# The second gathered quad of each pair waits for later products instead of the sum that frees its slot

## The chip, the core and the metric

The kernel runs on one core of one Trainium2 chip. The metric is the device time of one execution in microseconds (us), the median over several executions. TensorE (PE) multiplies matrices, VectorE (DVE) and ScalarE (ACT) work elementwise, GpSimd (POOL) here mostly issues gathers, SyncE (SP) issues the other DMAs.

## The reference, cut to what matters

A graph of 3125 nodes with 128 features and 50,000 edges goes through five gated steps and a normalisation, then through three edge layers and a second normalisation. The change lies in the edge layers, of which each does this:

```python
parts = [x[src], x[dst]]
if edge_attr is not None:
    parts.append(edge_attr)
e = relu(concatenate(parts, axis=-1) @ We + be)
agg = segment_sum(e * norm[:, None], dst, num_segments=3125)
x_new = relu(concatenate([x, agg], axis=-1) @ Wn + bn)
```

`edge_attr` is absent in the first edge layer and is the previous layer's `e` in the second and third. The last layer's `e` isn't needed by anybody.

## The kernel before

The products with the nodes' features are made once a layer (`p` for the source side, with the bias, `q` for the target side), so that an edge needs one row of `p`, one row of `q` and, from the second layer on, its own `e` times a 128x128 matrix. `edge_pass` then walks over the edges. An edge tile holds 128 edges, a quad is four tiles, and a pass has 115 quads, each in a slot of its own, numbered in order of time. Two kinds of quads alternate:

- 43 **sorted** quads: their rows of `p` come out of SBUF by a one-hot matmul (L1592).
- 72 **rest** quads, number `b` = 0 to 71: their rows of `p` are gathered from DRAM by GpSimd, four indirect DMAs a quad, one a tile, into one of `ROW_SLOTS` = 4 buffers `rows`, number `b % 4` (L1512).

The order of slots is sorted, rest, rest, over and over (36 triples), with one more sorted quad after every fifth triple, seven in all. So the rest quads come in pairs: an even `b`, called the first of a pair here, and an odd one, the second, in the next slot.

For the quad in slot `q`, TensorE does `products(q)`: the one-hot matmuls with `q_parts` (L1599), for a sorted quad the one with `p_sb` (L1592), and in the second and third pass the matmul with `before` (L1603). Its last matmul raises `spread`. For a rest quad VectorE adds the gathered rows (`add`, L1737; it waits for `spread` and for the gather's landing), ScalarE applies the relu (L1677). Two slots later TensorE does `turn_and_sum(q)`: in the first two passes it turns `e` for storing (L1614), and always it multiplies `e` by the weighted one-hot matrix (L1623); the last matmul raises `summed`. VectorE takes the sums into `agg_t` in `gather_up` (L1744). The order on TensorE is written out by hand:

```python
products(q, values)
if q >= LAG:
    turn_and_sum(q - LAG)
```

with `LAG` = 2. `summed` is therefore the last reader of a `rows` buffer, and GpSimd waits for it before it gathers the quad `b` into the buffer of `b - 4`. The first four quads of a pass wait for less. Each engine's instructions are executed in order; GpSimd's four gathers of a quad follow the wait without another. SyncE loads `before`, stores `after` and loads the rows for the sorted quads meanwhile.

Of the kernel before, what the change touches and what calls it, by code (L numbers as in the profile page):

```python
# [1370 lines left out]
def edge_pass(nc, tag, nth, Wc, psum, keep, t, is_first, p_dram, e_before, e_after, over_before,  # L1371
# [4 lines left out]
    with ExitStack() as ctx:  # L1376
# [3 lines left out]
        def sem(name):  # L1380
            return ctx.enter_context(nc.semaphore(name + tag))
# [3 lines left out]
        ROWS, BEFORE, AFTER, LOADED, PAIRS, OWN = ROW_SLOTS, 3, 3, 2, 2, 2  # L1385
# [29 lines left out]
        spread = sem("spread")  # L1415
# [45 lines left out]
        def slot_of(b):  # L1461

            return rest_slots[b]

        def lists(i, first, engine):

            end = 4 * QUAD if i < TRIPLES else 2 * QUAD
            _, values = nc.values_load_multi_w_load_instructions(
                keep["list_i"][0:1, i, first:end], engines=(engine,), min_val=0, max_val=WINDOWS - 1,
                skip_runtime_bounds_check_because="a window's number is a count of at most all the windows but one")  # L1470
            return values

        def overflow(engine):

            return nc.values_load(keep["over_i"][0:1, 0:1], engines=(engine,), min_val=0,
                                  max_val=ALL_TILES - SORT_TILES)
# [15 lines left out]
        @block.gpsimd  # L1492
        def _(pool):
            def further_rows():
                with pool.Fori(0, overflow(mybir.EngineType.Pool)) as i:
                    pool.wait_ge(over_hots_on, i * 4 + 4)
                    pool.sem_inc(over_gathering, 1)
                    nc.gpsimd.indirect_dma_start(
                        out=over_row, out_offset=None, in_=p_dram,
                        in_offset=bass.IndirectOffsetOnAxis(ap=over_src[:].bitcast(U32), axis=0),  # L1500
                    ).then_inc(over_row_in, 16)

            for b in range(REST_QUADS):
                if b == 1:
                    further_rows()
                if b >= ROWS:
                    pool.wait_ge(summed, slot_of(b - ROWS) + 1)
                elif b >= 2:
                    pool.wait_ge(spread, slot_of(b - 2))
                for m in range(QUAD):  # L1510
                    s = b * QUAD + m
                    nc.gpsimd.indirect_dma_start(  # L1512
                        out=rows[:, b % ROWS, m * D:(m + 1) * D], out_offset=None, in_=p_dram,
                        in_offset=bass.IndirectOffsetOnAxis(ap=t["src_i"][:, s:s + 1].bitcast(U32), axis=0),
                    ).then_inc(rows_in[b % ROWS], 16)
# [313 lines left out]
```

## Time and profile before

| what | us |
|---|---|
| median of 3 executions | 2675.99 |
| fastest and slowest of them | 2674.0 and 2693.58 |
| the profiled execution's own time | 2685.29 |
| span of its profile, first to last instruction | 2683.2 |

The profile comes from one execution, 9.3 us above the median. Its span begins with the tables, the adjacency and the gated steps, which the change doesn't touch. The three edge passes lie at about 962 to 1488, 1519 to 2066 and 2098 to 2640 us. In a timeline an instruction has its start, its duration, and in brackets the idle time of its engine just before it and what ended that. "remote" there is a semaphore whose raiser the profile doesn't name, "issue" is a time in which the engine waited for nothing that the profile shows. The end of a matmul is modelled.

### The profile page before, as it was taken

The numbers are of one execution on the slowest core, as the hardware profiler recorded it, in microseconds if no ns is written. First come the engines' busy times: TensorE is split into PE (matmuls) and PEld (weight loads), VectorE is DVE, ScalarE is ACT, GpSimd is POOL, SyncE is SP. The second block draws the span as 40 slices with busy tenths as digits, with TensorE's granted clock in tenths as the row PEclk, the third lists the DMA queues.
The fourth block names the chain that finished last, engine by engine and source line by source line (L and its number), as shares of the span: only waits on it lengthen the run. The fifth ranks groups of instructions, "written<-read, shape, count | busy, mean of one in ns | idle before, by whom it ended". The sixth has DMA issues, their size and how long they took to land. (4 is left out here: it accounts for less than half of the span.)

```text
span 2683.2 us, 48362 instructions
## 1 busy us (share of the span) xinstructions
PE 2142.4 (80%) x14264; PEld 1585.6 (59%) x14264; DVE 1447.8 (54%) x4661; ACT 653.0 (24%) x1271; POOL 1001.1 (37%) x1015
## 2 busy tenths in 40 slices
PE   7666679999999657777777678888888677888885
PEld 4222234444444347666666578787877577777774
DVE  6988832332332446656666455555555455555555
ACT  0246731221221122222222322222222211111111
POOL 0765400000000035555555245454553454555550
PEclk8777789999999768878888899999999888889887
DMA  2123550000000343333333255555553333433431
GB/s 81 25 57 83 95 47 1 0 0 0 0 0 0 120 127 107 116 102 114 105 112 108 83 164 160 154 164 165 162 162 117 103 101 97 112 105 106 112 106 38
DMA packets 193650, 242.15 MB, mean 90 GB/s; under 512 B 56276, under 2 KB 120047, under 8 KB 192799
## 3 DMA queue, kind: packets, MB, share of 16 engines
q1 hardware_dynamic: 161023, 172.73, 22.3%
q0 software_dynamic: 31840, 57.21, 9.1%
q10 hardware_dynamic: 576, 9.44, 0.9%
q8 instruction: 128, 2.10, 0.3%
q14 instruction: 83, 0.68, 0.1%
HBM read 149.75 MB, written 69.88 MB: 82 GB/s over the span
## 5 line engine op out<-in xcount | busy, mean ns | idle before, releaser
L1512 POOL DMA_INDIRECT rows<-p_dram,src_i x864 | 824.7, 954 | 751.9 <-PE psum L1623 441.8
L1744 DVE TENSOR_TENSOR agg_t<-psum,agg_t 128x128 f32 x1380 | 394.1, 286 | 466.6 <-remote 263.6
L1603 PE MATMUL psum<-w_c,before 128*128 128x128 f32 x1840 | 440.8, 321 | 24.2 <-issue 23.8
L1592 PE MATMUL psum<-p_sb,pair_src 128*128 x1032 | 257.7, 330 | 151.3 <-issue 85.6
L1677 ACT ACTIVATE rows<-rows 128x512 f32<-128x512 f32 x216 | 136.1, 630 | 901.1 <-DVE rows L1737 608.3
L893 PE MATMUL psum<-adj,parts 128*128 (+2 forms) x1750 | 339.7, 351 | 5.8 <-ACT agg L972 4.4
L1603 PEld LDWEIGHTS psum<-w_c,before 128*128 128x128 f32 x1840 | 305.3, 207 | 27.4 <-issue 27.3
L1728 DVE TENSOR_SCALAR hot_w<-col_f,dst_loc,weight 128x128 f32<-128x128 f32 x864 | 308.5, 360 | 0.5
L1623 PE MATMUL psum<-hot_w,rows 128*128 128x128 f32 x1728 | 279.8, 307 | 29.4 <-issue 27.6
L1592 PEld LDWEIGHTS psum<-p_sb,pair_src 128*128 128x128 f32 x1032 | 188.2, 224 | 175.7 <-issue 173.6
L1599 PE MATMUL psum<-q_parts,hot_all 128*128 x2592 | 270.2, 229 | 15.5 <-issue 15.4
L1623 PEld LDWEIGHTS psum<-hot_w,rows 128*128 128x128 f32 x1728 | 255.8, 223 | 38.9 <-issue 37.5
L1599 PE MATMUL psum<-q_parts,pair_dst 128*128 x1548 | 213.7, 244 | 74.9 <-issue 74.1
L893 PEld LDWEIGHTS psum<-adj,parts 128*128 128x128 f16 x1750 | 153.0, 98 | 191.3 <-issue 23.4
L672 PE MATMUL psum<-src_hot,dst_hot 128*128 128x391 f16 x586 | 196.6, 441 | 87.0 <-DVE src_hot L653 41.8
L1737 DVE TENSOR_TENSOR rows<-psum,rows 128x512 f32<-128x512 f32 x216 | 148.3, 686 | 193.2 <-remote 180.8
L1599 PEld LDWEIGHTS psum<-q_parts,hot_all 128*128 128x128 bf16 x2592 | 217.0, 104 | 30.9 <-issue 20.1
L1266 POOL MEMSET agg_t<- 128x3200 f32 x1 | 2.8, 2764 | 616.4 <-POOLq L1029 616.4
L1599 PEld LDWEIGHTS psum<-q_parts,pair_dst 128*128 128x128 bf16 x1548 | 153.0, 112 | 107.7 <-issue 94.6
L841 DVE SCALAR_TENSOR_TENSOR gate_room<-psum,b_h,gate_room 128x512 f32<-128x512 f32 (+1 forms) x35 | 23.9, 683 | 348.1 <-ACT gate_room L979 348.1
L672 PEld LDWEIGHTS psum<-src_hot,dst_hot 128*128 128x128 f16 x586 | 59.0, 101 | 224.7 <-issue 224.7
L634 POOL DMA_INDIRECT records<-record_of,place_i x128 | 158.5, 1239 | 88.3 <-PE psum L672 67.2
(241 smaller groups left out, 2590.4 us busy)
## 6 DMA issues: line engine op xcount, KB each, us to landing
e_dram<-after SPq DMA_DIRECT2D x230, 256.0 KB
before<-e_dram SPq DMA_DIRECT2D x230, 256.0 KB
adj<-stage SPq DMA_DIRECT2D x196, 97.8 KB
pair_rows<-sorted_rows SPq DMA_DIRECT2D x129, 128.0 KB
rows<-p_dram,src_i POOLq DMA_INDIRECT x864
hot_all<-dst_rows ACTq DMA_DIRECT2D x2, 3072.0 KB, 15.0
p_dram<-p_sb SPq DMA_DIRECT2D x6, 384.0 KB
records<-record_of,place_i POOLq DMA_INDIRECT x128
```

The source lines that it names most:

```text
L634: nc.gpsimd.indirect_dma_start(out=keep["records"], out_offset=bass.IndirectOffsetOnAxis(ap=keep["place_i"][:, s:s + 1].bitcast(U32), axis=0),
L672: nc.tensor.matmul(psum[:, bass.ds(bank, 1), 0:SPAN], dst_hot[:, s // HOT_BATCH % BATCHES, s % HOT_BATCH, :], src_hot[:, s % MOVES, 0:SPAN ...
L893: mm = nc.tensor.matmul(psum[:, AGG_BANK, 0:n_cols], parts[:, w, part, :], adj[:, w, cols], start=(w == 0 and part == 0), stop=(w == WINDO ...
L1512: nc.gpsimd.indirect_dma_start(out=rows[:, b % ROWS, m * D:(m + 1) * D], out_offset=None, in_=p_dram, in_offset=bass.IndirectOffsetOnAxis( ...
L1592: nc.tensor.matmul(o, pair_src[:, i % PAIRS, m, :], t["p_sb"][:, bass.ds(values[m], 1), :], start=True, stop=False)
L1599: mm = nc.tensor.matmul(o, hot, t["q_parts"][:, bass.ds(window, 1), part, :], start=(part == 0 and i is None), stop=(part == 2 and e_befor ...
L1603: mm = nc.tensor.matmul(o, before[:, q % BEFORE, m * P:(m + 1) * P], w_c[:], start=False, stop=True)
L1623: mm = nc.tensor.matmul(psum[:, A_BANKS[q % len(A_BANKS)], m * P:(m + 1) * P], e[:, m * D:(m + 1) * D], hot_w[:, q % (LAG + 1), m, :], sta ...
L1677: nc.scalar.activation(e_of(q), source, ACT.Relu).then_inc(e_on, 1)
L1728: nc.vector.tensor_scalar(hot_w[:, q % (LAG + 1), m, :], keep["col_f"][:], of, weight, ALU.is_equal, ALU.mult).then_inc(hot_on, 1)
L1737: nc.vector.tensor_tensor(row, psum[:, E_BANKS[q % len(E_BANKS)], 0:WIDE], row, ALU.add).then_inc(added, 1)
L1744: nc.vector.tensor_tensor(a, psum[:, A_BANKS[q % len(A_BANKS)], m * P:(m + 1) * P], a, ALU.add).then_inc(agg_on, 1)
```

## The change

In `edge_pass` the wait ahead of the four gathers of a second quad (odd `b`, from 5 on) is another. Its slot less one is the slot of quad `b - 1`, which tells it from a first quad. Before, it waited until the sum of quad `b - 4` was made, the quad that had its buffer. Now it waits until `products` of the slot three further on than that of `b - 4` is made. For most pairs this is the second rest quad of the next triple, quad `b - 2`. TensorE makes these products after that sum, so the buffer is free then.

```diff
@@ -1503,7 +1503,9 @@
             for b in range(REST_QUADS):
                 if b == 1:
                     further_rows()
-                if b >= ROWS:
+                if b >= ROWS and slot_of(b) - 1 == slot_of(b - 1):
+                    pool.wait_ge(spread, slot_of(b - ROWS) + 4)
+                elif b >= ROWS:
                     pool.wait_ge(summed, slot_of(b - ROWS) + 1)
                 elif b >= 2:
                     pool.wait_ge(spread, slot_of(b - 2))
```

No instruction is added, taken away or moved. On GpSimd in the first pass, quads 3, 4 and 5 (four indirect DMAs each, the first with the wait) stood like this before:

```order
 L1512 DMA rows_0<-p_dram,src_i 128x128 [waits spread_0]
 L1512 DMA rows_0<-p_dram,src_i 128x128 x3
 L1512 DMA rows_0<-p_dram,src_i 128x128 [waits summed_e_0]
 L1512 DMA rows_0<-p_dram,src_i 128x128 x3
 L1512 DMA rows_0<-p_dram,src_i 128x128 [waits summed_e_0]
 L1512 DMA rows_0<-p_dram,src_i 128x128 x3
```

and stand like this now:

```order
 L1514 DMA rows_0<-p_dram,src_i 128x128 [waits spread_0]
 L1514 DMA rows_0<-p_dram,src_i 128x128 x3
 L1514 DMA rows_0<-p_dram,src_i 128x128 [waits summed_e_0]
 L1514 DMA rows_0<-p_dram,src_i 128x128 x3
 L1514 DMA rows_0<-p_dram,src_i 128x128 [waits spread_0]
 L1514 DMA rows_0<-p_dram,src_i 128x128 x3
```

Only quad 5's wait differs, and so every second one from there on. Quad 3's wait for `spread` is one of those at a pass's start and is the same in both. `spread_0` and `summed_e_0` are the first pass's `spread` and `summed`. Between the old and the new releaser TensorE has the work of one quad's products. The place where it stands, in the first pass, is the end of one `turn_and_sum` (L1614, L1623) and the start of the products of a rest quad (L1599):

```order
 L1614 MATMUL psum<-ident,rows_0 128x128 [waits after_on_0,e_on_0]
 L1614 MATMUL psum<-ident,rows_0 128x128 x3
 L1623 MATMUL psum<-hot_w_0,rows_0 128x128 [waits agg_on_0,hot_on_0]
 L1623 MATMUL psum<-hot_w_0,rows_0 128x128 x3
 L1599 ISA [waits hot_t_on_0,added_0]
 L1599 MATMUL psum<-q_parts,hot_all 128x128
```

The last row of the sum raised the semaphore that GpSimd waited for; now the last of the twelve L1599 matmuls behind it raises the one that counts. TensorE's own order is as it was.

## Rows read from the trace of the kernel before

**Rows 1.** The page: each engine's busy time, and the group of the gathers.

```profile
PE 2142.4 (80%) x14264; PEld 1585.6 (59%) x14264; DVE 1447.8 (54%) x4661; ACT 653.0 (24%) x1271; POOL 1001.1 (37%) x1015
...
L1512 POOL DMA_INDIRECT rows<-p_dram,src_i x864 | 824.7, 954 | 751.9 <-PE psum L1623 441.8
```

**Rows 2.** Passes: length, busy PE, PEld, DVE, ACT, POOL, granted clock, DMA share, GB/s.

```profile
962.00:1488.00 526.00, 386.49 (x3111) 351.36 (x3111) 316.85 (x1151) 126.99 (x234) 275.95 (x289) 0.81 0.37 112
1519.00:2066.00 547.00, 454.45 (x4033) 420.53 (x4033) 298.39 (x1077) 132.41 (x234) 275.00 (x289) 0.94 0.54 157
2098.00:2640.00 542.00, 435.70 (x3572) 399.56 (x3572) 299.00 (x1077) 72.66 (x118) 276.53 (x289) 0.87 0.38 103
```

**Rows 3.** Timeline of GpSimd in the third pass: first and last gathers of quads.

```profile
2369.56 0.94 POOL L1512 DMA_INDIRECT rows<-p_dram,src_i  x1 [6.19 <-PE psum L1623]
...
2373.30 0.94 POOL L1512 DMA_INDIRECT rows<-p_dram,src_i  x1 [0.30 <-issue]
2375.53 0.94 POOL L1512 DMA_INDIRECT rows<-p_dram,src_i  x1 [1.29 <-PE psum L1623]
...
2381.92 1.13 POOL L1512 DMA_INDIRECT rows<-p_dram,src_i  x1 [1.71 <-PE psum L1623]
...
2385.91 0.94 POOL L1512 DMA_INDIRECT rows<-p_dram,src_i  x1 [0.30 <-issue]
2387.16 0.94 POOL L1512 DMA_INDIRECT rows<-p_dram,src_i  x1 [0.30 <-issue]
...
2397.53 0.94 POOL L1512 DMA_INDIRECT rows<-p_dram,src_i  x1 [5.62 <-PE psum L1623]
```

**Rows 4.** Stretches from one first quad's gathers to the next's (columns of rows 2).

```profile
997.93:1013.35 15.42, 10.22 (x81) 8.98 (x78) 8.82 (x33) 3.20 (x6) 7.54 (x9) 0.80 0.31 97
1277.64:1289.85 12.21, 8.70 (x84) 7.70 (x80) 9.33 (x35) 2.91 (x6) 7.65 (x8) 1.00 0.46 143
1430.96:1446.07 15.11, 11.19 (x79) 10.21 (x79) 8.32 (x30) 3.90 (x8) 7.60 (x9) 0.73 0.31 97
1700.26:1713.37 13.11, 11.28 (x106) 10.21 (x104) 6.26 (x24) 3.42 (x6) 7.55 (x8) 1.00 0.64 179
1727.12:1744.85 17.73, 14.02 (x102) 12.71 (x102) 8.69 (x32) 3.42 (x6) 7.59 (x8) 0.81 0.46 144
2143.97:2160.70 16.73, 12.19 (x93) 11.42 (x91) 8.48 (x31) 1.94 (x4) 7.72 (x8) 0.81 0.36 101
2369.56:2381.92 12.36, 10.11 (x94) 9.28 (x94) 6.97 (x27) 1.67 (x3) 7.53 (x8) 1.00 0.38 98
2381.92:2397.53 15.61, 12.26 (x94) 11.12 (x92) 8.56 (x31) 2.05 (x4) 7.86 (x9) 0.78 0.34 99
```

**Rows 5.** Timeline of VectorE in the stretch of rows 3: sums taken, rows added.

```profile
2375.41 0.29 DVE L1744 TENSOR_TENSOR agg_t<-psum,agg_t 128x128 f32 x1 [3.08 <-PE psum L1623]
...
2377.23 0.69 DVE L1737 TENSOR_TENSOR rows<-psum,rows 128x512 f32<-128x512 f32 x1
...
2386.69 0.29 DVE L1744 TENSOR_TENSOR agg_t<-psum,agg_t 128x128 f32 x1 [1.64 <-remote]
...
2393.46 0.69 DVE L1737 TENSOR_TENSOR rows<-psum,rows 128x512 f32<-128x512 f32 x1 [4.87 <-remote]
```

**Rows 6.** Timeline of TensorE in the stretch of rows 3.

```profile
2370.93 1.06 PE L1623 MATMUL psum<-hot_w,rows 128*128 128x128 f32 x8
...
2383.26 1.06 PE L1623 MATMUL psum<-hot_w,rows 128*128 128x128 f32 x8
...
2385.65 0.44 PE L1603 MATMUL psum<-w_c,before 128*128 128x128 f32 x2
...
2390.52 0.37 PE L1592 MATMUL psum<-p_sb,pair_src 128*128 x1 [1.05 <-issue]
```

**Rows 7.** Line L1737, the adds of the gathered rows: what VectorE waited for.

```profile
L1737 DVE TENSOR_TENSOR rows<-psum,rows x216: 676/685/693, 984.6 to 2636.9; 128x512 f32<-128x512 f32 x108
...
  remote: 180.8, 50
```

## The prediction

> **What bounds the kernel now.** The page comes first: GpSimd is busy 37% of the span, and of its 751.9 us of idle time ahead of gathers 441.8 us end with the sum, L1623 [rows 1]. So the gathers are started by TensorE, and the changed wait is one that really holds GpSimd. Then the passes: they take 526, 547 and 542 us, TensorE is busy 386, 454 and 436 us of them, and the clock granted to it is 0.81, 0.94 and 0.87 of full speed [rows 2]. A pass whose matmuls are fewest (the first) isn't shorter in proportion, and TensorE runs part of the time at the lower of its two levels, 1.2 GHz for 2.4.
>
> Where that time goes shows in two neighbouring triples of the third pass [rows 3]. The first quad's gathers start at 2369.56, the last of the four ends at 2374.24, GpSimd waits 1.29 us, and the second quad's start at 2375.53; the next first quad's start at 2381.92. In the triple behind it the second quad starts at 2387.16, 0.30 us after the last gather of the first (2385.91 + 0.94): eight gathers in a row. The next first quad starts at 2397.53. The same matmuls (94 records each) took 12.36 us at a clock of 1.00 in the spaced triple and 15.61 us at 0.78 in the contiguous one [rows 4]. In the contiguous one TensorE pauses in the middle of a quad's products, where the code waits for nothing: 1.05 us ahead of one L1592 matmul [rows 6]. The products that ended at 2386.09 by the modelled end were taken by the add only at 2393.46, after 4.87 us of idle time [rows 5, 6].
>
> This repeats. I went through GpSimd's timeline pair by pair and sorted the pairs by the idle time ahead of the second quad. It is 0.3 to 0.5 us in 14 pairs of the first pass, in 1 of the second and in 12 of the third (quads 4 and up), and about 1.2 us or more in all others. From first quad to first quad, the first pass's contiguous triples take 14.3 to 15.4 us, 210.8 us for all 14; 15.42 and 15.11 are the first and the last of them. Spaced ones take 12.21. In the second pass it is 17.73 against 13.11. In the third the 12 take 194.4 us, from 15.5 to 16.7 (16.73 is the first), against 12.36 [rows 4]. Of the 180.8 us that the adds waited for "remote", in 50 waits, nearly all are the one wait of some 5 us that each contiguous triple has [rows 7].
>
> **The change, part by part.** Nothing is removed or added but the releaser of 34 waits in each pass.
>
> *The contiguous pairs.* A second quad starts at once when its sum is seen before the first quad's gathers end, some 4.7 to 4.9 us after they started. In the contiguous triple that sum's matmuls end at 2384.32, and VectorE took it at 2386.69, within 4.8 us of 2381.92 [rows 3, 5, 6]. Products of the next rest quad follow it. They run four times through three L1599 matmuls and one or two L1603 records; the block of which 2385.65 is the end comes 1.77 us after the sum by the modelled ends (2386.09 less 2384.32), and in the trace they were first seen at 2393.46. Without the second burst they would be seen near where the spaced triple sees things: there the sum was seen 5.8 us after the burst's start (2375.41 less 2369.56), the products not later than 7.7 us after it (2377.23) [rows 5]. Both are past 4.7 us. So I expect each contiguous pair of the second and third pass to become a spaced one. In the first pass the products have no L1603 and are about 0.8 us long, so the margin is thin: a sum seen at 4.2 gives products at 5.0 or more. I take it as enough.
>
> The prices then are: first pass 210.8 - 14 x 12.4 = 37 us. Second pass 17.7 - 13.3 = 4 us. Third pass 194.4 - 12 x 12.7 = 42 us. Together 83 us. I take 12.4, 13.3 and 12.7, a little above the spaced triples of rows 4, for the reason that follows.
>
> *The pairs already spaced.* Their second quad starts later by the time from seeing the sum to seeing the products. The trace bounds it by 0 below (what is seen late is often seen together) and by 1.8 us above (2377.23 less 2375.41, an upper bound since VectorE was busy) [rows 5]. Whether the triple gets longer depends on who starts the next first quad: it waits for a sum that comes two products and two sums later on TensorE, and GpSimd was idle for 1.71 us before 2381.92 [rows 3], so 1.4 us of delay fit in before the gathers themselves are late. But in the spaced triples first and second starts lie 5.97 and 6.39 us apart, and what TensorE finishes during a burst tends to be seen only some 5.8 us after its start, so part of the delay may be passed on. I take 0.1 us for each of some 39 spaced triples of the first two passes and 0.4 for 15 of the third: 10 us. The ends are 0 and 1.8 x 54 = 97 us.
>
> *The gathered rows' own deadline.* The second quad whose gathers begin at 2375.53 and end some 4.7 us later is quad 37 of the pass, and its add is the one at 2393.46, 13 us later [rows 3, 5]. That cover is far more than the delay of one quad's products. Without it each late microsecond would be paid in full.
>
> *The sum.* 2685.3 us of the profiled execution - 83 + 10 = 2612. That execution lies 9.3 us above the median of 2676.0, so against the median I predict **2603 us**, 2.7% less.
>
> Of the link between gathers and TensorE the trace shows a pause and a lower clock when eight gathers follow each other, and none of either with a gap of 1.3 us [rows 3, 4, 6]. The Trainium skill, SBUF — State Buffer, section "SBUF: two separate sides", says that engine ports and DMA ports are disjoint, that neither can slow the other, and that TensorE's reads wait for nobody. By it the pauses would have another cause, the spacing would buy nothing, and the time would stay at 2676; the trace doesn't bear that out so far, but it doesn't show the cause either.
>
> **The rivals.**
>
> *No effect.* The pause belongs to a phase of TensorE's work and makes the pair contiguous, not the other way round: a sum that is seen early starts the second quad early. For it: the same triple has both. Against it: the pause starts only after the second burst has, and the spaced and contiguous triples carry the same matmuls. Then only the delay of the spaced pairs is left: 2676 to 2686, the middle 2680. The rule of the page above would end here too.
>
> *Only the third and second pass gain.* The first pass's short products are seen before 4.7 us and its pairs stay contiguous. That leaves 46 - 10 = 36 us: 2640.
>
> *Slower: the contact moves to the other side.* The next first quad starts 6.39 us after the second in the spaced triple [rows 3]. If the new wait takes TensorE's work of one quad's products (1.8 us in the third pass) out of that stretch, 4.6 to 5.1 us are left, and four gathers take 5.0. Then the first quad follows the second without a gap and the eight in a row are back, one quad later. The price is the same, 2.9 us (first pass, 15.1 - 12.2) or 3.8 (third, 16.2 - 12.4) a triple. It undoes the whole gain when it strikes more than 73 / 3.3 = 22 of the some 66 triples of these passes. If it strikes two of three, 44, the time is 2603 + 44 x 3.3 = 2748; I put it at 2720 with a little over half. Against it: what TensorE finishes in a burst is mostly seen 5.8 us after its start, which keeps the gap.
>
> *A larger gain.* Gaps of 1.3 us still leave short pauses in TensorE's records; with 2 us they may go too, 1 us a triple more, and the clock stays up: 2560.
>
> **How the numbers follow.** The main case has 0.60, from 2580 to 2630 by the ends of its terms. Only the later passes gain: 0.12. A larger gain: 0.06. No effect: 0.11. Slower: 0.11. A measurement of this kernel tells a change from none at about 1%, that is 26.8 us, so faster begins under 2649. Main, partial and larger gain lie there but for a small tail: 0.76. Same has 0.13 with that tail, slower 0.11. The range reaches up to 2668, into the no-effect case, and down to 2562.
>
> **What the changed profile would show.** Idle time ahead of second quads of 1.2 us or more nearly everywhere, ended by the products (L1601 or L1605 of the changed file) instead of the sum. The clock of the first and third pass above 0.81 and 0.87. Triples of 12 to 13 us without those of 15 to 17. Waits of the adds for "remote" down from 180.8 us to some 30. The prediction is wrong if the first quads are found to follow the second ones at 0.30 us, if spaced triples grow by over 1 us, or if the pauses stay where the gathers are spaced.

## The result, and the profile after

The changed kernel takes 2496.56 us (median of 3 executions, 2496.01 to 2496.61) against 2675.99. The ratio is 0.933, with an interval of 0.929 to 0.937. I had predicted 2603, with a range from 2562 to 2668: the direction is right, and the gain of 179 us is 2.5 times the 73 that I forecast.

One thing has to be known to read the rest. The kernel before runs at one of two levels, and a whole job (all executions of one session on a chip) is at one of them. In the pair above and in three later jobs it took 2676, 2670, 2668 and 2672 us; in four other jobs 2229, 2228, 2229 and 2231. It isn't the chip alone: one and the same chip gave 2228 and 2229 in two jobs and 2672 in a third. I call them the upper and the lower level. Each run is compared only with the kernel before in its own job.

The page of the changed kernel, the lines that answer to [rows 1] and [rows 7]:

```profile
PE 2020.9 (81%) x14264; PEld 1486.9 (60%) x14264; DVE 1452.6 (58%) x4661; ACT 652.7 (26%) x1271; POOL 1006.2 (40%) x1015
...
L1514 POOL DMA_INDIRECT rows<-p_dram,src_i x864 | 828.7, 959 | 580.0 <-issue 201.1
...
L1739 DVE TENSOR_TENSOR rows<-psum,rows 128x512 f32<-128x512 f32 x216 | 147.8, 684 | 70.0 <-remote 66.3
```

GpSimd idles 580.0 us ahead of gathers instead of 751.9, the adds wait 66.3 us for "remote" instead of 180.8 (a semaphore whose raiser the profile doesn't name), and TensorE's busy time has fallen by 121.5 us with the same 14264 matmuls. Its windows over the three passes, cut where those of [rows 2] are cut, with the same columns:

```profile
962.00:1433.00 471.00, 351.23 (x3111) 318.53 (x3111) 318.68 (x1149) 128.36 (x233) 277.36 (x289) 0.91 0.43 125
1463.00:1953.00 490.00, 426.66 (x4033) 403.95 (x4033) 300.90 (x1080) 130.03 (x234) 276.57 (x289) 0.97 0.60 176
1984.00:2453.00 469.00, 378.51 (x3572) 351.38 (x3572) 301.46 (x1079) 72.67 (x118) 277.01 (x289) 0.98 0.44 119
```

The passes are 55, 57 and 73 us shorter, and the granted clock rose from 0.81, 0.94 and 0.87 to 0.91, 0.97 and 0.98. GpSimd's timeline in the third pass shows the new rhythm, to be held against [rows 3]:

```profile
2212.01 0.95 POOL L1514 DMA_INDIRECT rows<-p_dram,src_i  x1 [1.41 <-remote]
...
2215.76 0.97 POOL L1514 DMA_INDIRECT rows<-p_dram,src_i  x1 [0.30 <-issue]
2218.13 0.95 POOL L1514 DMA_INDIRECT rows<-p_dram,src_i  x1 [1.40 <-remote]
...
2224.28 0.98 POOL L1514 DMA_INDIRECT rows<-p_dram,src_i  x1 [1.44 <-remote]
...
2230.41 0.95 POOL L1514 DMA_INDIRECT rows<-p_dram,src_i  x1 [1.40 <-remote]
```

Every quad now starts 6.1 us behind the one before, with 1.4 us of idle time, first and second alike. TensorE in the same stretch has one pause of over 1 us a quad, and it ends at the same distance from the first gather each time, 5.64, 5.71 and 5.68 us:

```profile
2214.24 1.06 PE L1625 MATMUL psum<-hot_w,rows 128*128 128x128 f32 x8
...
2217.65 0.40 PE L1605 MATMUL psum<-w_c,before 128*128 128x128 f32 x2 [1.19 <-issue]
...
2223.84 0.47 PE L1605 MATMUL psum<-w_c,before 128*128 128x128 f32 x2 [1.13 <-issue]
...
2229.96 0.39 PE L1605 MATMUL psum<-w_c,before 128*128 128x128 f32 x2 [1.14 <-issue]
```

The first line is the sum that the quad at 2218.13 waits for. By the modelled ends it was made at 2215.30, GpSimd was idle from 2216.73 on, and yet it started 1.4 us later. So by these ends the gap isn't there because TensorE still has work to do for it; what TensorE has finished is seen late. Over all passes, where GpSimd was idle ahead of a quad, it started 2.8 us (first quads) and 2.9 us (second quads) in the median after the modelled end of what it waited for.

From GpSimd's timelines of both kernels I took the start of every first quad from 4 on, 33 triples a pass, and sorted them by what they were before:

| triples, by kind before | pass 1 | pass 2 | pass 3 | gain, us |
|---|---|---|---|---|
| eight gathers in a row | 14: 210.8 to 172.2 | 1: 17.7 to 12.3 | 12: 194.5 to 147.1 | 91.3 |
| spaced | 13: 160.8 to 159.0 | 26: 348.4 to 324.2 | 15: 186.3 to 183.7 | 28.7 |
| with an extra sorted quad | 6: 88.8 to 79.9 | 6: 114.9 to 93.5 | 6: 100.2 to 81.9 | 48.7 |

They make 168.7 us. The spans differ by 2683.2 - 2494.5 = 188.7. Of the 20 that are left, 16 lie in the passes, ahead of and behind these triples, and 4 outside the passes. By the engines' lines of the two pages, 121.5 of the 188.7 us are less busy time of TensorE for the same matmuls, which goes with the higher clock; only the other 67 are less idle time.

### The profile page after: what moved, and what is told of

Read it like the earlier page. It is cut to its first block and busy times, and to the rows that moved or that the text cites. A ratio compares the mean times of both kernels' runs of the same rounds, so it can differ in the third digit from the quotient of the medians.

```text
span 2494.5 us, 48362 instructions
## 1 busy us (share of the span) xinstructions
PE 2020.9 (81%) x14264; PEld 1486.9 (60%) x14264; DVE 1452.6 (58%) x4661; ACT 652.7 (26%) x1271; POOL 1006.2 (40%) x1015
## 5 line engine op out<-in xcount | busy, mean ns | idle before, releaser
L1605 PE MATMUL psum<-w_c,before 128*128 128x128 f32 x1840 | 413.6, 305 | 32.5 <-issue 32.4
L1594 PE MATMUL psum<-p_sb,pair_src 128*128 x1032 | 227.3, 302 | 115.3 <-issue 39.7
L1605 PEld LDWEIGHTS psum<-w_c,before 128*128 128x128 f32 x1840 | 283.6, 193 | 39.0 <-issue 38.9
L1601 PE MATMUL psum<-q_parts,hot_all 128*128 x2592 | 274.2, 225 | 35.4 <-issue 34.9
L1730 DVE TENSOR_SCALAR hot_w<-col_f,dst_loc,weight 128x128 f32<-128x128 f32 x864 | 301.5, 352 | 0.5
L672 PE MATMUL psum<-src_hot,dst_hot 128*128 128x391 f16 x586 | 197.2, 439 | 86.2 <-issue 38.0
L1625 PE MATMUL psum<-hot_w,rows 128*128 128x128 f32 x1728 | 241.4, 285 | 5.0 <-issue 4.9
L1601 PEld LDWEIGHTS psum<-q_parts,hot_all 128*128 128x128 bf16 x2592 | 213.1, 102 | 53.3 <-issue 42.4
L1594 PEld LDWEIGHTS psum<-p_sb,pair_src 128*128 128x128 f32 x1032 | 163.6, 199 | 133.6 <-issue 131.2
L1625 PEld LDWEIGHTS psum<-hot_w,rows 128*128 128x128 f32 x1728 | 222.5, 201 | 8.4 <-issue 8.4
L1601 PE MATMUL psum<-q_parts,pair_dst 128*128 x1548 | 183.1, 224 | 31.4 <-issue 29.8
L672 PEld LDWEIGHTS psum<-src_hot,dst_hot 128*128 128x128 f16 x586 | 58.8, 100 | 224.7 <-issue 224.7
L1739 DVE TENSOR_TENSOR rows<-psum,rows 128x512 f32<-128x512 f32 x216 | 147.8, 684 | 70.0 <-remote 66.3
L1730 DVE TENSOR_SCALAR hot_w<-col_f,record_of 128x128 f32<-128x128 f32 x516 | 181.9, 358 | 11.4 <-PEq L151 11.2
## 6 DMA issues: line engine op xcount, KB each, us to landing
hot_all<-dst_rows ACTq DMA_DIRECT2D x2, 3072.0 KB, 15.1
```

The source lines that it names most:

```text
L672: nc.tensor.matmul(psum[:, bass.ds(bank, 1), 0:SPAN], dst_hot[:, s // HOT_BATCH % BATCHES, s % HOT_BATCH, :], src_hot[:, s % MOVES, 0:SPAN ...
L1594: nc.tensor.matmul(o, pair_src[:, i % PAIRS, m, :], t["p_sb"][:, bass.ds(values[m], 1), :], start=True, stop=False)
L1601: mm = nc.tensor.matmul(o, hot, t["q_parts"][:, bass.ds(window, 1), part, :], start=(part == 0 and i is None), stop=(part == 2 and e_befor ...
L1605: mm = nc.tensor.matmul(o, before[:, q % BEFORE, m * P:(m + 1) * P], w_c[:], start=False, stop=True)
L1625: mm = nc.tensor.matmul(psum[:, A_BANKS[q % len(A_BANKS)], m * P:(m + 1) * P], e[:, m * D:(m + 1) * D], hot_w[:, q % (LAG + 1), m, :], sta ...
L1730: nc.vector.tensor_scalar(hot_w[:, q % (LAG + 1), m, :], keep["col_f"][:], of, weight, ALU.is_equal, ALU.mult).then_inc(hot_on, 1)
```

## The experiments at the lower level

Theory A is that of the prediction: eight gathers in a row make TensorE pause, and the change cures that by spacing them. The first four kernels ran in one job, which turned out to be at the lower level (2228.69 us for the kernel before, where the expectations reckon with 2676), so that they tell what the kernel does when the pauses are absent, and don't test theory A.

**Wider gap** (`landed`). The wait of before stays, and the second quad also waits for the first one's rows:

```diff
                 if b >= ROWS:
                     pool.wait_ge(summed, slot_of(b - ROWS) + 1)
+                    if b % 2:
+                        pool.wait_ge(rows_in[(b - 1) % ROWS], 16 * QUAD * (nth * (REST_QUADS // ROWS) + (b - 1) // ROWS + 1))
```

> The second quad waits for the sum as before, and besides for the landing of the first quad's gathers; TensorE's products play no part. If it is the spacing of the two quads' gathers that counts (theory A), every gap becomes some 1.3 us, no triple of 15 us or more is left, and the time is near the changed kernel's 2496.6 (2480 to 2530). If it is the releaser that counts, that the second quad starts only when TensorE has got one quad's products further (theory B), the pairs that were contiguous gain a little, since TensorE stands where it stood, and the time is 2580 to 2680.

2528.11 us, ratio 1.136 (1.133 to 1.138). The gaps of 2.4 to 4.0 us add to GpSimd's own 10 us a triple.

**Only the first quad later** (`first_late`), the reverse of the change:

```diff
-                if b >= ROWS:
+                if b >= ROWS and b % 2 == 0:
+                    pool.wait_ge(spread, slot_of(b - ROWS) + 4)
+                elif b >= ROWS:
                     pool.wait_ge(summed, slot_of(b - ROWS) + 1)
```

> The first quad of each pair gets the later wait in place of the second, which keeps its own. TensorE reaches the second quad's sum soon behind those products, so that nearly all pairs are contiguous. Theory A: every triple costs what the contiguous ones of the kernel before cost (15.1, 17.7 and 16.2 us in the three passes), some 75 more such triples by 2.9 to 4.4 us, 2900 us (2830 to 3000). Theory C, that a later start of any gather relieves TensorE: faster than before, 2500 to 2650.

2254.73 us, ratio 1.012 (1.010 to 1.014), with every pair a row of eight.

**A short filler** (`filler_half`), ahead of the second quad's unchanged wait:

```diff
+                if b >= ROWS and b % 2:
+                    nc.gpsimd.memset(filler[:, 0:512], 0.0).then_inc(filled, 1)
+                    pool.wait_ge(filled, (b - ROWS) // 2 + 1)
```

(The scratch buffer and its semaphore are declared elsewhere and left out here, as in the later edits with a filler.)

> GpSimd fills 512 columns of a scratch buffer (some 0.5 us with its own semaphore) after the first quad's gathers, ahead of the second quad's unchanged wait for the sum. Contiguous pairs get a gap of some 0.8 to 0.9 us, less than a landing takes. Theory A with any gap: near 2500. Theory A with the landing as the threshold: the pauses stay, only a little shorter, 2640 to 2700. Theory B: 2640 to 2700.

2270.36 us, ratio 1.019 (1.017 to 1.021).

**Hardly any gathers** (`no_gathers`). Only the first four quads of a pass are gathered, later adds read old rows. Their wait for the gathers' landing is taken out too, which isn't shown:

```diff
-            for b in range(REST_QUADS):
+            for b in range(ROWS):
```

> Only the first four quads of each pass are gathered; the later adds take what stands in the buffers, so the output is another and 272 of 288 gathers of a pass are left out. It shows TensorE's own pace. If all pauses and the low clock come from the gathers, the triples take some 8.5, 12 and 10.6 us by the matmuls' records, and the whole 2676 minus some 130 + 65 + 85 and the changed kernel's rest: 2330 to 2420. If the pauses are TensorE's own, the time stays above 2600.

2192.34 us, ratio 0.984: at this level the gathers cost 36 us in all.

Then the two kernels as they are, in a second job:

> The kernel before, unchanged, for its profile on this job's chip. Where it takes 2229 us: GpSimd gathers at 10.0 us a triple with gaps of 0.3 us and TensorE has next to no pauses. Where it takes 2676: as in the rows shown, gaps of 0.3 and 1.2 us and pauses behind the short ones.

> The changed kernel beside the kernel before, on the chip of this job. Where the kernel before takes 2229 us, its gathers follow each other without pauses of TensorE (the mirrored kernel, whose quads all touch, took 2255 there and not the 2900 of theory A). So theory A needs a condition that the chip brings: what TensorE finishes during a burst is seen late on one chip and at once on another. If this job's chip shows the kernel before near 2229, the changed kernel is within 1.5% of it (2215 to 2260). If it shows it near 2676, the changed kernel is near 2497. A rival, that the changed kernel has a cost or gain of its own whatever the chip, asks for a ratio of 0.93 on both.

Before 2227.62, changed 2228.82, ratio 1.000 (0.999 to 1.002). At the lower level the change does nothing, and spacing can only cost. The trace of the kernel before at this level (span 2220.9 us) shows why. The same eight gathers in a row, three windows as in [rows 2], and three groups of its lines:

```profile
1957.65 0.94 POOL L1512 DMA_INDIRECT rows<-p_dram,src_i  x1 [0.30 <-issue]
...
1967.68 0.95 POOL L1512 DMA_INDIRECT rows<-p_dram,src_i  x1 [0.31 <-issue]
```

```profile
927.00:1312.00 385.00, 319.38 (x3111) 301.02 (x3111) 316.93 (x1152) 125.37 (x234) 278.09 (x289) 0.93 0.51 153
1342.00:1762.00 420.00, 402.42 (x4033) 395.33 (x4033) 299.98 (x1081) 128.91 (x234) 276.32 (x289) 0.97 0.71 205
1794.00:2179.00 385.00, 358.94 (x3572) 350.46 (x3572) 299.84 (x1078) 72.47 (x118) 276.71 (x289) 0.96 0.53 145
```

```profile
L1512 POOL DMA_INDIRECT rows<-p_dram,src_i x864 | 828.3, 959 | 345.8 <-issue 247.2 <-PE psum L1623 66.6 <-POOLq L151 31.7
...
L1603 PE MATMUL psum<-w_c,before 128*128 128x128 f32 x1840 | 410.9, 305 | 0.0
...
L1623 PE MATMUL psum<-hot_w,rows 128*128 128x128 f32 x1728 | 231.3, 277 | 0.0
```

All 99 second quads follow their first at 0.3 us here. The triples take 10.1 to 10.2 us in the median, and eight gathers take 8 x 1.25 = 10.0: GpSimd is the bound of the first and the third pass, where nearly every first quad follows at 0.3 us too. A gather takes as long as at the upper level (959 ns against 954 in [rows 1]); what is missing is TensorE's idle time.

A third job, also at the lower level (2228.83), and a fourth (2231.47):

> From the fifth rest quad of each pass on, each of the four gathers is replaced by one GpSimd memset of 128x960 float32 with a semaphore of its own, so that GpSimd is busy about as long (some 1 us each) and no row is moved; the output is not the reference's. Where the kernel before takes 2676 us (triples of 15 to 17 us with two quads' gathers in a row). Theory A, eight gathers in a row make TensorE's updates arrive late: without gathers the pauses and the late updates are gone, triples of 10.0 to 10.5 us, 2230 us or less. Rival B, GpSimd being busy for 10 us is enough, whatever it does (an SBUF port or its own queue): triples stay at 15 us, 2600 to 2680. Where the kernel before takes 2228 us (triples of 10.1 us): if GpSimd's own time for eight gathers sets the triple of the first and third pass, as the 10.0 us of eight gathers at 1.25 us says, the time stays at 2215 to 2235; if the moved rows set it, it falls towards the 2192 us of the kernel without gathers.

The adds' wait is changed as in `no_gathers`.

```diff
+                    if b >= ROWS:
+                        nc.gpsimd.memset(filler[:, 0:960], 0.0).then_inc(filled, 1)
+                        pool.wait_ge(filled, (b - ROWS) * QUAD + m + 1)
+                        continue
```

2260.66 us, 1.4% more than before, where I had expected no change. These memsets slow VectorE: the adds of the rows take 776 ns for 686, the weighted one-hots of the rest quads (L1734, L1728 before) 651 for 357, and VectorE is busy 359 us of the 418 after the first pass's start instead of 334. That cost is this edit's own.

> The changed kernel with six buffers for gathered rows in place of four, so that a quad's gathers wait for a quad two further back and all waits come loose. Where the kernel before takes 2676 us: theory A says that loose waits put the gathers in one row without a gap, eight and more, and bring the late updates back: triples of 14 to 17 us or worse, 2650 us or more. The rival, that the length of a triple is set by the waits for sums on a slow link and not by gathers in a row, says faster than the changed kernel, 2450 us or less. Where the kernel before takes 2228 us: GpSimd's gathers set the first and the third pass, so a looser wait buys little: 2215 to 2230; if instead its idle time ahead of the gathers counts, 2190 to 2210.

```diff
-ROW_SLOTS = 4
+ROW_SLOTS = 6
```

2224.60 us, ratio 0.998 (0.996 to 0.999). No other version that computes the reference was ahead of the kernel before here, and this one is by 0.2%.

> The changed kernel once more, on whichever chip this job gets, to see whether the kernel before takes 2676 us or 2228 us there. If the first pair's state of things is that of a chip and this is such a chip: before 2676, changed 2497, ratio 0.933. If it was a state of that one job: before 2228, changed 2229, ratio 1.00. A third possibility is a time between, with triples between 10.1 and 12.3 us.

2230.73 us, ratio 0.999 (0.998 to 1.001), on a third chip.

> Each indirect gather of the edge layers is replaced by a plain DMA of the same 128x128 block size, also issued by GpSimd, from consecutive rows; the output is not the reference's. Where before takes 2228 us: GpSimd's time for an issue sets the triple of the first and third pass (eight times 1.25 us), and a plain issue should be shorter than 0.94 us busy, so 2190 to 2225, near the 2192 of the kernel without gathers; if the moved bytes set the triple instead, 2225 to 2235. Where before takes 2676 us: theory A with the moved rows as the cause says still 2600 or more, theory A with the descriptors made by GpSimd as the cause says 2300 or less.

```diff
-                    nc.gpsimd.indirect_dma_start(
-                        out=rows[:, b % ROWS, m * D:(m + 1) * D], out_offset=None, in_=p_dram,
-                        in_offset=bass.IndirectOffsetOnAxis(ap=t["src_i"][:, s:s + 1].bitcast(U32), axis=0),
-                    ).then_inc(rows_in[b % ROWS], 16)
+                    nc.gpsimd.dma_start(rows[:, b % ROWS, m * D:(m + 1) * D], p_dram[s % 24 * P:(s % 24 + 1) * P, :]
+                                        ).then_inc(rows_in[b % ROWS], 16)
```

2191.09 us, as without gathers. An issue takes 0.55 us here, so GpSimd is no bound.

## The experiments at the upper level

The filler ran in a job at the upper level (2670.26 for the kernel before):

> The kernel before with a GpSimd memset of 128x512 float32 (some 0.5 us, with a semaphore of its own) ahead of each second quad's wait from quad 5 on, which spaces the two quads' gathers without changing what they wait for. It ran before where the kernel before takes 2228 us, and took 2270 us there. Where the kernel before takes 2676 us: theory A, that the row of eight gathers is what costs, says that a gap of 0.8 us cures a part or all of it, 2480 to 2620; the rival, that the changed wait cured something by its own place in TensorE's order, says 2676 or more. Where it takes 2228 us again: 2265 to 2275 as before.

2604.31 us, 2.5% less (one execution each). The same 0.5 us of idle work that cost 2% at the lower level gains here, without a change in what the quads wait for. The triples average 13.1, 13.0 and 14.0 us; no second quad follows its first at once any more, and the clocks (0.81, 0.96 and 0.86 in windows cut like those of [rows 2]) have hardly risen. How wide the gap is decides the rest. In 29 triples (without those with an extra sorted quad) it is only the filler's own 0.8 us, and they take 13.7, 14.5 and 15.5 us in the three passes, against 15.1, 17.7 and 16.2 without a gap before. In 51 it is over 1.5 us, and they take 12.5, 12.8 and 12.6, close to the changed kernel's 12.3, 12.5 and 12.3. So a gap of 0.8 us cures a part and a wider one nearly all, with the old wait. (The widths weren't set by the edit but came about by the waits; this compares triples within one run.)

Four kernels ran in the next job (2668.1 for the kernel before):

> The first quad of each pair waits for products one quad later than it needs and the second waits for its sum as before, so that only the first quad's start moves. Where the kernel before takes 2670 us: theory A, that eight gathers in a row cost 3 to 4 us a triple, says 2700 to 2900, since the second quad's start then follows the first at once in all triples; the rival, that every triple is two bursts of gathers with TensorE's updates seen only at their ends, whichever quad waits for which, says 2500 to 2620, near the changed kernel, if the late first quad breaks the rows of eight as well. Where before takes 2228 us: 2255 again.

2943.4 us, ratio 1.102 (1.091 to 1.113): 10% slower, more than theory A's 2700 to 2900 and far from the rival's 2500 to 2620, where the same edit cost 1.2% at the lower level. Every pair is a row of eight, and the triples take 15.4, 17.5 and 16.5 us in the three passes, as those with a row of eight did in the kernel before (15.1, 17.7 and 16.2). Two neighbouring ones in the third pass, and TensorE in the first of them:

```profile
2513.69 0.94 POOL L1514 DMA_INDIRECT rows<-p_dram,src_i  x1 [6.43 <-PE psum L1605]
...
2522.43 0.94 POOL L1514 DMA_INDIRECT rows<-p_dram,src_i  x1 [0.30 <-issue]
2529.34 0.94 POOL L1514 DMA_INDIRECT rows<-p_dram,src_i  x1 [5.96 <-PE psum L1605]
```

```profile
2518.78 0.33 PE L1601 MATMUL psum<-q_parts,pair_dst 128*128 x3
2519.37 0.36 PE L1605 MATMUL psum<-w_c,before 128*128 128x128 f32 x1 [0.26 <-issue]
2520.09 0.27 PE L1605 MATMUL psum<-w_c,before 128*128 128x128 f32 x1 [0.35 <-issue]
2520.80 0.37 PE L1625 MATMUL psum<-hot_w,rows 128*128 128x128 f32 x1 [0.44 <-issue]
2521.51 0.27 PE L1625 MATMUL psum<-hot_w,rows 128*128 128x128 f32 x1 [0.34 <-issue]
2522.23 0.59 PE L1625 MATMUL psum<-hot_w,rows 128*128 128x128 f32 x3 [0.44 <-issue]
2524.34 0.37 PE L1625 MATMUL psum<-hot_w,rows 128*128 128x128 f32 x1 [1.53 <-issue]
2525.05 0.60 PE L1625 MATMUL psum<-hot_w,rows 128*128 128x128 f32 x2 [0.33 <-issue]
2525.44 0.53 PE L1601 MATMUL psum<-q_parts,hot_all 128*128 x3
```

Up to 5.4 us after the first gather TensorE runs without a pause (2518.78 + 0.33 less 2513.69). From 5.7 us on it does one matmul record about every 0.71 us (a float32 matmul leaves two, 1840 for the 920 of L1603), and it runs freely again at 2525.44, 2.1 us after the last gather ended (2522.43 + 0.94 = 2523.37). From there its matmuls take longer (0.53 for three where 0.33 stood); the clock of the whole stretch is 0.81. A quad's four gathers have ended when that begins; eight reach far into it.

> The changed kernel beside the kernel before. If this job again has a chip where the kernel before takes 2670 us: 2497 and a ratio of 0.933, as in the first pair; the state then belongs to some chips and comes again. Otherwise 2229 and 1.00.

2496.61 us, ratio 0.934 (0.927 to 0.941). The first result repeats.

> Plain DMAs issued by GpSimd, of the same block size and number, in place of the indirect gathers; the output is not the reference's. Where the kernel before takes 2670 us: if it is GpSimd's long indirect instructions that keep TensorE's updates from being seen, 2192 to 2300, since a plain issue takes 0.55 us; if it is the number of software DMAs or the moved rows, TensorE's pauses stay and it takes 2450 or more. Where before takes 2228 us: 2191 again.

2220.31 us where the kernel before takes 2668: plain DMAs of the same bytes take nearly all of the upper level away (2191 at the lower). The pauses are gone from TensorE's groups:

```profile
L1512 POOL DMA_DIRECT2D rows<-p_dram x864 | 465.3, 547 | 640.9 <-PE psum L1621 587.4 <-POOLq L151 31.1 <-issue 14.4
...
L1601 PE MATMUL psum<-w_c,before 128*128 128x128 f32 x1840 | 408.6, 304 | 0.0
...
L1597 PE MATMUL psum<-q_parts,hot_all 128*128 x2592 | 252.5, 220 | 0.0
```

> GpSimd memsets of 128x960 in place of the gathers from the fifth rest quad of each pass on, no rows moved; the output is not the reference's. Where the kernel before takes 2670 us: theory A says no pauses of TensorE above those at the passes' starts, 2260 to 2300, as on the other chips; rival B (GpSimd being busy is enough) says 2600 or more. Where before takes 2228 us: 2260 again.

2302.25 us: a GpSimd that is as busy, without gathers, disturbs little either (2261 at the lower level). What is left of a difference, 29 and 42 us in these two, lies mostly ahead of the first pass: it begins at 962 and 966 us here, at 962 in before, and at 928 and 927 at the lower level. So neither the moved bytes alone nor GpSimd's being busy makes the pauses; the indirect DMAs do. The plain ones differ in three things, the kind of instruction, its 0.55 us for 0.95, and rows that lie side by side in DRAM; which of them matters is open.

The last three ran in one more job (2672.12):

> The changed kernel with a GpSimd memset of 128x512 (with a semaphore of its own, a gap of some 0.8 us in place of 0.3) between the second and the third gather of each quad from the fifth on, so that a burst is two gathers. On a chip where the kernel before takes 2670 us: if TensorE's pauses and late updates last only as long as gathers follow each other, the updates pass in the middle gap too, triples of 11.1 to 12.0 us (GpSimd alone needs 8 x 1.25 + 2 x 0.52 = 11.0) and 2390 to 2480. If they are seen only once four gathers are over, whatever the gap, the memset comes on top: 13.3 us a triple, 2570 to 2620. Where before takes 2228 us: GpSimd's own time, 11.0 us a triple, 2270 to 2310.

```diff
+                    if b >= ROWS and m == 2:
+                        nc.gpsimd.memset(filler[:, 0:512], 0.0).then_inc(filled, 1)
+                        pool.wait_ge(filled, b - ROWS + 1)
```

2513.13 us, ratio 0.940 (0.936 to 0.944). Neither expectation holds. The triples stay at 12.2, 12.6 and 12.2 us; the gap in the middle took time from the gaps between the quads, which fell from 1.4 us to 0.3 to 1.3 in the median, and the time didn't fall. One thing speaks for theory A: 33 of the 99 second quads follow their first at 0.3 us, and yet their triples aren't long (12.3, 12.8 and 12.2 us in the means of the passes, for the 24 without an extra sorted quad). With the gap in the middle of each quad these are rows of four.

> The second quad of a pair waits also until the first quad's gathers have landed, which puts 2 to 4 us between them. Where before takes 2670 us: no row of eight is left, so theory A says faster than before; the gap costs GpSimd's time, and by the 2528 us that it took where before takes 2228 it cannot be under some 2528. I expect 2530 to 2640. If wide gaps let TensorE run without a pause, 2530; if the late updates come on top of the wider gap, 2600 and more.

2585.41 us, ratio 0.967 (0.961 to 0.974), inside what was expected. The triples take 13.0, 13.7 and 13.0 us. A wider gap beats rows of eight within the pair, but in 35 of the 99 triples the next first quad now follows the second at 0.3 us: the contact has moved to the other side, as my slower rival had it for the change itself.

> The changed kernel with six buffers for gathered rows in place of four; all waits of the gathers come loose by two quads. Where before takes 2670 us: theory A says that nothing keeps the quads' gathers apart any more, rows of eight and more come back, 2600 to 3000. The rival, that waits for sums set the triple, says 2450 or less. Where before takes 2228 us: 2225 again.

2523.73 us, ratio 0.944 (0.940 to 0.948). Both expectations missed, theory A's 2600 to 3000 and the rival's 2450 or less: with six buffers the rows of eight don't come back. The gaps are 1.3 to 1.6 us in the median, as with four, and a quad again starts some 2.8 us after the modelled end of what it waits for. Why looser waits keep that gap isn't shown. No version that computes the reference was faster than the changed one at the upper level.

A part of TensorE's idle time for "issue" may be waits whose semaphore record is missing from the trace. So here are only its pauses of over 0.15 us inside a block of products, of transposes or of sums, where the code waits for nothing, over the three passes of each trace:

| kernel | time, us | pauses | their sum, us |
|---|---|---|---|
| before, upper level | 2685 | 352 | 206 |
| changed | 2497 | 240 | 151 |
| `first_late_2`, all pairs in a row | 2942 | 486 | 335 |
| `filler_again` | 2604 | 301 | 168 |
| `landed_2` | 2579 | 285 | 171 |
| `six_after_2` | 2520 | 256 | 162 |
| `split` | 2509 | 271 | 122 |
| `pool_busy_2`, hardly any gathers | 2302 | 4 | 5 |
| `plain_pool_2`, plain DMAs | 2220 | 0 | 0 |
| before, lower level | 2223 | 0 | 0 |

The times are those of the profiled executions. `split` has the shortest pauses of the versions with gathers and isn't the fastest; its memsets take GpSimd's time, and its clocks are 0.86, 0.96 and 0.93 in the three passes.

## Why the prediction was right in direction and wrong in size

*The contiguous pairs*: right. 26 of the 27 rows of eight are gone, the first pass's thin margin held, and the term measured 91.3 us for 83. `first_late_2` (all in a row, +10%), `after_slow` (next to none, -6.6%) and the widths of the gaps in `filler_again`, where the waits are the old ones, show that the row is the cause. The cause is tied to the upper level: `after_again` and `after_third` have the same edit without effect.

*The reading behind the sum* failed first. I wrote that the trace shows a pause and a lower clock when eight gathers follow each other "and none of either with a gap of 1.3 us", and so priced both in the contiguous triples alone. The spaced triple of [rows 3] itself has pauses, 2.2 us in five of them, the last in the middle of a sum:

```profile
2381.24 0.41 PE L1623 MATMUL psum<-hot_w,rows 128*128 128x128 f32 x2 [0.83 <-issue]
```

Two terms were wrong by it.

*The pairs already spaced*: a failed step. I wrote that "part of the delay may be passed on" and booked a cost of 10 us. It was a gain of 28.7, of which 24.2 in the second pass. Two neighbouring first quads there, before and after:

```profile
1567.84 1.01 POOL L1512 DMA_INDIRECT rows<-p_dram,src_i  x1 [2.50 <-PE psum L1623]
...
1573.79 0.94 POOL L1512 DMA_INDIRECT rows<-p_dram,src_i  x1 [1.20 <-remote]
...
1581.15 0.94 POOL L1512 DMA_INDIRECT rows<-p_dram,src_i  x1 [2.67 <-PE psum L1623]
```

```profile
1509.78 0.95 POOL L1514 DMA_INDIRECT rows<-p_dram,src_i  x1 [1.52 <-PE psum L1625]
...
1515.93 0.95 POOL L1514 DMA_INDIRECT rows<-p_dram,src_i  x1 [1.45 <-remote]
...
1522.20 0.95 POOL L1514 DMA_INDIRECT rows<-p_dram,src_i  x1 [1.55 <-PE psum L1625]
```

The second quad starts 0.2 us later (6.15 after the first for 5.95), and the next first one 1.1 us earlier (6.27 for 7.36). TensorE's idle time for "issue" in such a triple of before is 0.58, 0.69 and 1.09 us, the last of them ahead of this row, 5.7 us after the second quad's first gather:

```profile
1579.50 0.49 PE L1614 MATMUL psum<-ident,rows 128*128 128x128 f32 x3 [1.09 <-issue]
```

In the triple of the changed kernel 0.26, 0.44 and 0.67 us are left, and none lies some 5.7 us behind the second quad's first gather. The 26 spaced triples of the second pass bear it out: the pauses inside blocks fell from 1.44 to 0.61 us a triple in the mean. In the spaced triples of the first and third pass they stayed (1.84 to 1.73 and 1.85 to 1.87 us), and the gains there are small, 1.9 and 2.6 us in all. I reasoned with a fixed amount of work that TensorE still owed, but how much it pauses hangs on how the bursts lie; why only the second pass gained so is open. That a little more gap takes pauses away was in my text, as the rival of a larger gain, with a chance of 0.06, but for gaps of 2 us, where these went from 1.3 to 1.4.

*Triples with an extra sorted quad*: the larger failed step, a term left out of the sum without a reason. My 83 and 10 us cover 27 and 54 triples. The six others that I measured in each pass took 14.8, 19.2 and 16.7 us, and fell to 13.3, 15.6 and 13.7: 48.7 us that no term stood for. None of them has a row of eight, and their pauses inside blocks didn't shrink (0.8, 0.7 and 0.8 us before, 2.2, 1.2 and 1.8 after). It goes with the clock: the granted share in them was 0.84, 0.89 and 0.86 before and 0.98, 1.00 and 1.00 after, and TensorE's busy time fell from 13.3, 17.2 and 15.3 us to 11.0, 14.3 and 11.8. I had taken the lower clock for a matter of the contiguous triples. What lowered it in these isn't shown; the second pass had only one row of eight.

*The rest of the span*, 20 us, had no term either. The misses add up: 8 + 39 + 49 + 20 = 116, and 73 + 116 = 189. That is the difference of the two profiled executions; the one before lay 9.3 us above its median, so that the medians differ by 179.

*The gathered rows' deadline*: right as far as the trace names it, no wait of an add is put down to a gather. They still wait 66.3 us for "remote", where I said some 30; whose semaphore that was isn't shown.

*The rivals.* "No effect" fell at this level. At the other the time did stay the same, but not for that rival's reason: there are no pauses to take away. Nothing in the one trace could tell that. The rule of the Trainium skill beside it (SBUF — State Buffer, section "SBUF: two separate sides") isn't contradicted as to ports: the plain DMAs write as many blocks of the same size into the same buffers, and TensorE has no pause. What I drew from it, that the spacing would buy nothing, was wrong: the pauses don't come with the moved blocks, and they do hang on the spacing. "The contact moves to the other side" didn't happen: the idle time ahead of first quads is 1.4 to 1.6 us in the median, and the triples of `first_late_2` show what it would have cost.

*What the changed profile would show*: gaps of 1.2 us or more, yes, but the idle time ahead of gathers is put down to "remote" 141 times, to L1625 48 times, and to L1605 or L1601 only 16 times. Clocks up, yes. Triples of 12 to 13 us, yes (12.3, 12.5, 12.3).

## What stays open

What sets the level of a job. At both levels the gated steps, which have no gathers, run alike: from 400 to 700 us TensorE is busy 293.45 us before at the upper and 292.25 at the lower, both at a clock of 1.00. The sorting at the kernel's start, where GpSimd also issues indirect DMAs, is slower at the upper level: its matmuls L672 wait 34.2 us for "issue" there and 0.4 at the lower. So the level shows only where indirect DMAs are issued, as far as these stretches tell.

How the gathers hold TensorE up. That it runs for some 5 us and then one matmul at a time looks like an engine that lives on instructions it holds and whose supply is held up while such DMAs are made. No run tests it, and two things in the traces speak against it as the whole story. The packets of the queue q8, of the kind "instruction" (128 of them, 2.10 MB), take 0.99 us each in the median of the passes at both levels. And what TensorE has already finished is seen late as well: where VectorE was idle ahead of taking a sum (L1744), it took it 3.0 us in the median after the modelled end of that sum's matmuls at the upper level, 0.15 us at the lower.

What the recording has to do with it. At the upper level about half of the semaphore records are missing from the trace: 18,102 for the kernel before, against 36,874 at the lower level, with the same number of instructions; beside plain DMAs nearly all are there (35,077 in `plain_pool_2`). In the gated steps from 400 to 700 us both have 302. That is also why "remote" stands only in traces of the upper level. Whether the records get lost by the same hold-up, or whether writing them is a part of it, no run tells apart.

## What to carry to other kernels

When a busy engine pauses without a wait in the code, and only while another engine issues a row of indirect DMAs, break the row: place the wait so that each burst ends before the pause begins (here bursts of 4.7 us, a pause from 5.7 us on, and gaps of 1.4 us), and look at every kind of iteration, the rare ones too, when you sum the gain. Cost it by whole periods of the loop, and with the clock: of the gain here, 121.5 of 188.7 us were less busy time for the same matmuls, some of it in triples that had no row of eight. And measure in more than one session before you call such a gain the kernel's: here the same edit is worth 6.7% or nothing.

## What the hardware showed unexpectedly

The same kernel took 2228 or 2672 us on one and the same chip, by job. Beside gathers of 0.95 us each, issued every 1.25 us, TensorE at the upper level went down to one matmul every 0.71 us from 5.7 us after the first until 2.1 us after the end of the last; beside plain DMAs of the same size, issued in 0.55 us, it had no pause inside a block at all. And what it had finished was seen some 3 us late.
